# A graph network's rounds on one Trainium2 core: casting and splitting a batch of messages one step earlier, and one-hots and weights ahead between the rounds

## The reference

```python
x = layernorm(x + sage(x))   # 3 x: segment_sum(h[src], dst)/max(cnt,1) @ Wl + bl + h @ Wr, relu between
x = layernorm(x + gin(x))    # segment_sum(gelu(x[src] + edge_attr @ bond_W + bond_b) * ew, dst) + (1+eps)*x, then an MLP 128-256-128
x = layernorm(x + gcn(x))    # 2 x: segment_sum(norm * (h @ W)[src], dst) + self loop + b, relu, layer_norm * g + be
x = layernorm(x + rgcn(x))   # 2 x: segment_sum((h @ W[type])[src], dst) + h @ loop_w + b, relu between
```

## Time and profile before

| | us |
|---|---|
| runs of the kernel: median of 3 | 6575.37 (6567.12 to 6603.21) |
| the profiled execution | 6578.35 |
| its span | 6576.5 |
| rounds 0, 1, 2 (SAGE), by windows | 669, 523, 778 |
| round 3 (GIN) | 895 |
| rounds 4, 5 (GCN) | 748, 983 |
| rounds 6, 7 (RGCN) | 965, 1015 |
| busy in the span: PE, PEld, DVE, ACT, POOL | 4754.8, 3068.4, 3341.3, 2416.9, 1892.9 |

### The profile page before, as it was taken

One profiled execution on the slowest core, in us unless ns is written; L12 is line 12 of the kernel. 1 busy time (PEld: TensorE's weight loads), 2 busy tenths in 40 slices (PEclk: granted clock), 3 DMA queues, 4 the chain that ended last, 5 costly groups with the idle time before them and its releaser, 6 DMA issues. The chain is left out here.

```text
span 6576.5 us, 128477 instructions
## 1 busy us (share of the span) xinstructions
PE 4754.8 (72%) x25114; PEld 3068.4 (47%) x25115; DVE 3341.3 (51%) x10494; ACT 2416.9 (37%) x4967; POOL 1892.9 (29%) x1886
## 2 busy tenths in 40 slices
PE   5879578555577888956676666676788886777776
PEld 3445344222344555534443334342666663666663
DVE  3334233344554555546666566665344442566666
ACT  1333233133325777625554344443122222122223
POOL 4440652443204333034420432200322211322210
PEclk9989889777788999978888788888899999898899
DMA  3543465244323444334442344332233323233323
GB/s 99 160 154 134 154 193 189 94 126 128 127 94 122 142 140 143 128 100 137 137 127 91 113 130 131 123 124 92 88 103 104 98 97 113 84 97 98 100 91 100
DMA packets 429800, 789.83 MB, mean 120 GB/s; under 512 B 69304, under 2 KB 75250, under 8 KB 429716
## 3 DMA queue, kind: packets, MB, share of 16 engines
q1 hardware_dynamic: 375060, 671.58, 30.3%
q0 software_dynamic: 54656, 117.32, 7.2%
HBM read 480.10 MB, written 308.53 MB: 120 GB/s over the span
## 5 line engine op out<-in xcount | busy, mean ns | idle before, releaser
L1048 PE MATMUL p_agg<-onehot,msg 128*128 128x512 f16 (+1 forms) x2848 | 1217.2, 427 | 983.6 <-DVE onehot L1456 685.6
L642 POOL DMA_INDIRECT raw<-node_s,src_i x980 | 937.0, 956 | 2125.9 <-DVE msg L1447 952.7
L1456 DVE TENSOR_SCALAR onehot<-iota,dst_f,negbase 128x512 f16<-128x512 f16 (+1 forms) x2848 | 1063.1, 428 | 639.3 <-issue 232.8
L1050 PE MATMUL p_agg<-onehot,msg 128*128 128x512 f16 (+1 forms) x2848 | 1223.4, 430 | 0.5 <-issue 0.4
L1048 PEld LDWEIGHTS p_agg<-onehot,msg 128*128 x2848 | 292.2, 103 | 1385.4 <-issue 1258.3
L1447 DVE TENSOR_TENSOR msg<-raw,msg x140 | 163.1, 1165 | 728.5 <-ACT msg L763 660.0
L1507 DVE BATCH_NORM_STATS2 stats<-v_ring 128x6 f32 (+1 forms) x1960 | 429.1, 280 | 202.2 <-ACT v_ring L841 94.0
L642 POOL DMA_INDIRECT raw<-node_x,src_i x392 | 380.2, 970 | 430.0 <-issue 421.4
L833 ACT ACTIVATE o<-v_ring,nmr,rstd 128x128 f32 (+1 forms) x1176 | 472.2, 482 | 65.0 <-DVE nmr L1523 53.7
L803 ACT ACTIVATE u<-p_agg,sage_bias 128x512 f32<-128x512 f32 x196 | 133.8, 683 | 795.3 <-PE p_agg L1081 434.7
L1434 DVE SCALAR_TENSOR_TENSOR hid<-type_in,p_wide 128x512 f32<-128x512 f32 x448 | 253.2, 615 | 333.3 <-PE p_wide L1028 205.4
(11 more groups left out here) (258 smaller groups left out, 7953.6 us busy)
## 6 DMA issues: line engine op xcount, KB each, us to landing
node_s<-o SPq DMA_DIRECT2D x392, 256.0 KB
feature<-u SPq DMA_DIRECT2D x294, 256.0 KB
h_in<-feature SPq DMA_DIRECT2D x294, 256.0 KB
node_x<-o SPq DMA_DIRECT2D x294, 256.0 KB
res_in<-node_x SPq DMA_DIRECT2D x294, 256.0 KB
h_in<-node_x SPq DMA_DIRECT2D x196, 256.0 KB
h_in<-node_s SPq DMA_DIRECT2D x196, 256.0 KB
h_t<-dinv_scratch SPq DMA_DIRECT2D x196, 256.0 KB
```

What stands on the lines that cost most here:

```text
L642: nc.gpsimd.indirect_dma_start(out=raw[:, (e % RING) * BATCH + j, :], out_offset=None, in_=src_d, in_offset=bass.IndirectOffsetOnAxis(ap=s ...
L1048: nc.tensor.matmul(p_agg[:, a, :], tile_ap(msg, t, 0, D), oh, start=first, stop=True, skip_group_check=True)
L1050: return nc.tensor.matmul(p_agg[:, a, :], tile_ap(msg, t, D, 2 * D), oh, start=False, stop=True, skip_group_check=True)
L1456: return V.tensor_scalar(tile_ap(onehot, slot), iota[:, :], dst_f[:, bass.ds(t, 1)], negbase[:, bass.ds(it * 2 + a, 1)], ALU.subtract, ALU ...
```

## The change

It alters the order of work; every computation on data stays.

- In the SAGE and GCN rounds ScalarE casts at the head of step `it` the batches of pair `it + 2` instead of `it + 1`, and VectorE splits them at the end of step `it`; pair 1's batches are taken in step 0 too. TensorE's program has a wait for the early batches in all rounds. The list's word now counts on at most three batches a step (`AHEAD`); for these data the words stay as they are. GIN and RGCN keep the place of their batches.
- `onehots` is parted: `first_onehots` (the three of each half) and `more_onehots`. The additional groups of a pair's second half move to the head of VectorE's next step (`next_items`).
- Between the rounds VectorE waits for TensorE's last sums of the round before (`out_done`) and then makes the first six one-hots, before the first batch is split.
- SyncE loads the weights of rounds 3 to 7 ahead of the last store of the round before (`next_weights`), and GIN's 14 bond loads at the start of round 1. The first load of GIN's edge attributes goes ahead of `all_stored`.
- GpSimd hands batch 1 over ahead of the gathers of batch 2.
- In the GCN rounds ScalarE takes `relu_out` of both halves of the last pair ahead of `scale_rows`.

```diff
@@ words and lists
-        def even_list(eng, kind, row):
-
-            items, (first, second, third) = pair_list(eng, kind, row)
-            return (batch_in_word(eng, first), batch_in_word(eng, third)), items
+        def later_list(eng, kind, row):
+
+            items, (first, second, third) = pair_list(eng, kind, row)
+            return (batch_in_word(eng, second), batch_in_word(eng, first), batch_in_word(eng, third)), items
...
-        def batch_list(eng, kind, it):
-
-            end, begin = packed(words[0:1, bass.ds(it * 2 + 1, 2)], kind)
+        def batch_list(eng, kind, pair):
+
+            end, begin = packed(words[0:1, bass.ds(pair * 2 - 1, 2)], kind)
@@ SyncE
+                def next_weights():
+
+                    if r + 1 == len(rounds) or rounds[r + 1].kind == SAGE:
+                        return
+                    wait(sp, q.rows_done, NHALF)
+                    if k == 4:
+                        wait(sp, q.gained, NPAIR)
+                    for dst_ap, src_ap in round_weights(rounds[r + 1]):
+                        sp.dma_start(dst_ap, src_ap).then_inc(R[r + 1].weights_in, 16)
...
                 load(0, 0)
                 load(0, 1)
+                if r == 1:
+                    for dst_ap, src_ap in bond_weights:
+                        sp.dma_start(dst_ap, src_ap).then_inc(bond_in, 16)
...
-                for dst_ap, src_ap in round_weights(rd):
-                    sp.dma_start(dst_ap, src_ap).then_inc(s.weights_in, 16)
@@ GpSimd
-                    if e > 1:
+                    if e > 2:
                         hand_over(e - 1)
-                    elif e == 0:
-                        hand_over(0)
+                    elif e < 2:
+                        hand_over(e)
@@ ScalarE
                 def batches(it):
-                    if exists(it + 1):
-                        each_batch(act, *batch_list(act, PT, it), batch)
+                    if rel or k == 3:
+                        if exists(it + 1):
+                            each_batch(act, *batch_list(act, PT, it + 1), batch)
+                        return
+                    if is_zero(it):
+                        each_batch(act, *batch_list(act, PT, 1), batch)
+                    if exists(it + 2):
+                        each_batch(act, *batch_list(act, PT, it + 2), batch)
...
                 def step(it):
                     batches(it)
                     if k >= 4:
-                        relu_out(it - 1, 1)
+                        if not is_last(it - 1):
+                            relu_out(it - 1, 1)
                         deviation(it - 1)
+                        if is_last(it):
+                            relu_out(it, 0)
+                            relu_out(it, 1)
                         if k == 4:
                             scale_rows(it - 2)
@@ TensorE
-                if rel or k == 3:
-                    end = early_batches(pe, PT, batch)
-                    wait_apart(pe, q.lo_done, end * (1 + rel))
+                end = early_batches(pe, PT, batch if rel or k == 3 else None)
+                wait_apart(pe, q.lo_done, end * (1 + rel))
@@ VectorE
+                def next_items(it):
+
+                    if not exists(it + 1):
+                        if exists(it):
+                            more_onehots(it, 1, single_list(dve, PT, it * 2 + 1))
+                        return None, None, None
+                    if rel or k == 3:
+                        these, (now, after) = odd_list(dve, PT, it * 2 + 1)
+                        each_batch(dve, *these, batch)
+                        ahead = None
+                    elif exists(it + 2):
+                        (e0, e1, e2), (now, after) = later_list(dve, PT, it * 2 + 1)
+                        if is_zero(it):
+                            each_batch(dve, e0, e1, batch)
+                        ahead = (e1, e2)
+                    else:
+                        now, after = pair_list(dve, PT, it * 2 + 1)[0]
+                        ahead = None
+                    more_onehots(it, 1, now)
+                    return after[:3], after[3], ahead
...
                 def gcn_step(it):
-                    if exists(it + 1):
-                        these, (now, after) = even_list(dve, PT, it * 2 + 2)
-                        each_batch(dve, *these, batch)
-                        onehots(it + 1, 0, now)
+                    now, after, ahead = next_items(it)
+                    if now:
+                        onehots(it + 1, now)
                     scaled_sums(it, 1)
                     statistics(it - 1, 1)
                     gain_and_shift(it - 2)
-                    if exists(it + 1):
-                        onehots(it + 1, 1, after)
+                    if now:
+                        first_onehots(it + 1, 1, after)
                     scale_and_move(it - 1)
                     statistics(it, 0)
                     scaled_sums(it + 1, 0)
                     if k == 5:
                         second_scale_and_move(it - 2)
+                    batches_ahead(ahead)
...
+                if r:
+                    wait(dve, S[r - 1].out_done, NHALF)
+                now, after = pair_list(dve, PT, 0)[0]
+                first_onehots(0, 0, now[0])
+                first_onehots(0, 1, after[0])
                 if k == 3:
                     embedded_sum(0)
                 early_batches(dve, PT, batch)
-                now, after = pair_list(dve, PT, 0)[0]
-                onehots(0, 0, now)
-                onehots(0, 1, after)
+                more_onehots(0, 0, now)
```

More of the change, by code:

```diff
@@ L32 @@
 MORE = 2
+AHEAD = RING - 1
 REL = 8
@@ L325, in round_weights @@
                         (one_eps[:, :], rep("L1_gnn_eps"))]
-                for j in range(BATCH):
-                    out.append((bond[j * DE:(j + 1) * DE, j, :], A["L1_gnn_bond_W"]))
-                    out.append((bond[BATCH * DE:BATCH * DE + 1, j, :], A["L1_gnn_bond_b"].partition_broadcast(1)))
                 return out
@@ L345, in build_gnn @@
         sage_weights_in = sem("sage_weights_in")
+        bond_weights = [(bond[j * DE:(j + 1) * DE, j, :], A["L1_gnn_bond_W"]) for j in range(BATCH)]
+        bond_weights += [(bond[BATCH * DE:BATCH * DE + 1, j, :], A["L1_gnn_bond_b"].partition_broadcast(1))
+                         for j in range(BATCH)]
+        bond_in = sem("bond_in")
         shared = {name: sem(name) for name in StepSemaphores.NAMES}
@@ L357, in is_zero, with is_last @@
             return isinstance(it, int) and it == 0
+        def is_last(it):
+            return isinstance(it, int) and it == NPAIR - 1
         def exists(it):
@@ L476, in early_batches @@
             end = eng.snap(((word >> 24) & 31).with_bounds(min_val=1, max_val=BATCHES))
-            with eng.Fori(0, end) as e:
-                body(e.with_bounds(min_val=0, max_val=BATCHES - 1))
+            if body:
+                with eng.Fori(0, end) as e:
+                    body(e.with_bounds(min_val=0, max_val=BATCHES - 1))
             return end
```

54 lines of the change are left out of this document (35 added, 19 removed).

## The result

The changed kernel took 6479.84 us in the median of four runs (6458.47 to 6481.21), the kernel before 6571.24 us in runs beside it. The ratio is 0.9846 with a 95% interval from 0.9805 to 0.9887. The forecast was 6270 us, 305 us less than before; 91 us came by the medians, 97 by the spans of the two profiled executions.

What follows compares the result with a forecast made beforehand. No engine fills the batch cycles; VectorE's wait for ScalarE's cast and TensorE's for one-hots stand in them. 249 us for batches plus 56 around them, 305 us, gave 6270 us (chance 0.53), range 6110 to 6480.

Steps and rivals of the forecast that it cites:

- The cast and split ahead: Rounds 0, 1, 2, 4, 5: gains of 84, 39, 35, 10 and 81 us over 28 batches each, 249 us.
- The moved one-hot groups: Head of VectorE's next step, mostly last steps: adds and statistics go first; gain 12 us, between loss 12 and gain 30.
- The starts and batch 1: Round starts: first one-hots and weights earlier, 24 us; batch 1 handed over earlier in five rounds, 20 us.
- A: Rival: TensorE gets one-hots in time, but other engines see its results at GpSimd's scaling; gain 135 us, 6440 us; chance 0.21.
- the hold: While GpSimd gathers a batch, TensorE's completions reach other engines late, 5.9 us in round 2; the change only moves it.
- B: Rounds 2, 4, 5: GpSimd's scaling meets VectorE at every batch, 2.1 us each; 176 us less gain, 6446 us; chance 0.05.
- C: Rival: everything a batch costs in rounds 0, 1 and 5 goes, 403 us; 504 us in all, 6071 us; chance 0.10.
- D: Rival: ScalarE waits longer for matmuls at each batch, as GpSimd pauses less; 87 us slower, 6660 us; chance 0.07.
- E: Rival: batches aren't there when cast, ScalarE waits in VectorE's stead, only the starts gain; 6555 us; chance 0.04.

Runs made afterwards that it cites:

- e3: The kernel before with the cast and split ahead and nothing else; 6357.78 us, one run.
- e7: e1 with the gathers of batches 4 to 27 left out in the SAGE and GCN rounds, so it computes something else; 5968.93 us, one run.
- e6: e1 with the list read behind the copy of the first half's sum in SAGE, on another chip; 6240.77 us, 0.96 of the kernel before there.
- e10: The changed kernel itself, run again on a third chip; 6483.77 us, 0.9852 of the kernel before.
- e11: The kernel of e6, run again on a third chip; 6330.92 us, 0.9614 of the kernel before.
- e1: The changed kernel with the second half's additional one-hot groups back in their old place; 6320.53 us, 0.9611 of the kernel before.
- e5: The changed kernel with the moved groups at the end of VectorE's step, ahead of the list, on another chip; 6340.19 us, one run, 0.974 of the kernel before.
- e12: e11 with batch 1 handed over behind the gathers of batch 2 again; 6355.66 us, one run.
- e4: The kernel before with only the changes between rounds, batch 1's early handing over and the last pair's order in GCN; 6593.41 us, one run.

## Why the prediction was wrong

**The cast and split ahead.** The mechanism was right for the most part, as the waits and e3 show. The sum over 24 batches a round was near, 231 us measured (220 in e3) against 213 forecast, but that is luck, since the terms were off both ways; and for all 28 batches e3 has 214 against 249. For 24 batches I had 72, 34, 30, 9 and 70 us; measured were 47, 30, 31, 32 and 92. In round 0 TensorE's wait for one-hots did go, 3.4 us a batch, but the cycle is only (35.1 - 31.2)/2 = 2.0 us a batch shorter; unnamed waits came in its place, 229 us where there were 27. What the gathers cost in all e7 shows: round 0's cycle is 29.7 us with them (e6, same chip) and 26.1 without. In round 5 the forecast had it that the one-hots' stretching by the scaling "stays as it is". It fell by 34 us, which is more than the 22 that the term was short; its steps are 16.3 us in the mean, where a step without a batch was 15.49. In round 4 I took too much off the wait for the cast: 31 us came of the 75 that the wait held for 24 batches, where I had 9. Whether the list's reading of 1.68 us, which I subtracted, lay beside another wait, no run shows.

**The moved one-hot groups.** This is the step that failed. The forecast said that they "let the adds and statistics go first", a gain of 12 us between a loss of 12 and a gain of 30, since "no row has this by itself". They cost about 150 us: 153 between e10 and e11, 159 between the medians of the changed kernel and e1. The term was put at a gain of 12, and no rival had such a loss. I had asked whose work gets out of the queue's way, and not who waits for what is moved. TensorE takes the second half's groups at the beginning of its step; they were there already in the kernel before. With the groups at the head of VectorE's next step, TensorE waits until VectorE's whole step and the list are over (5.61 us in the timeline), and VectorE's next sum waits for TensorE. e5 parts the cost: in the last steps 57% is the list's reading ahead of the groups, in the whole time under half, the rest the place. It hits the rounds in which the groups bound the last steps, rounds 3 and 7 too, of which the forecast said that they stay as long as before, and not rounds 0, 1 and 6.

The price could have been bounded from rows that I had. The list was 1.68 us; as an estimate, a later group is late by that at least in each of the nine last steps, 76 us in the five rounds in which VectorE and TensorE turned out to work in turns, and 120 if it were all eight. I used that row for five other terms and not for this one.

**The starts and batch 1.** Forecast 24 + 20 us. The starts are 23 us shorter in the changed kernel, up to the fourth step mark, 15 of it in rounds 6 and 7. There e12 gives up to 17 us to batch 1, in rounds that I had left out of its term; in the five rounds for which I had 20 us it shows nothing. The six one-hots made ahead bring little, because the first batch is the bound. At the start of round 5 of the changed kernel, against the 3629.03 of the earlier trace rows:

```profile
3571.44 2.19 DVE L1486 TENSOR_SCALAR onehot<-iota,dst_f,negbase 128x512 f16<-128x512 f16 x6 [1.22 <-issue]
...
3577.11 0.95 ACT L785 ACTIVATE msg<-raw  x1 [16.81 <-POOL raw L726]
3578.42 1.09 DVE L1481 TENSOR_TENSOR msg<-raw,msg  x1 [4.78 <-ACT msg L785]
...
3580.75 0.61 PE L1081 MATMUL p_agg<-onehot,msg 128*128 128x512 f16 x1 [41.68 <-issue]
```

The one-hots are done 4.8 us before the split begins, and TensorE's first matmul comes 1.2 us after the split's end. What e4 lost in the middle of rounds 0 and 3 stays open in part, as said there.

**The rivals.** A (the hold takes what the cast gave) is true of a part: its sign, longer waits for a releaser not named, came in rounds 0 and 1, which gave 47 and 30 us all the same. B had a mechanism that is real, but with the wrong sign for this change: its full price, a one-hot of 2.4 us once a batch, stood in round 5 of the kernel before, and the change took most of it away. What is left is 0.36 us a batch. C's idea of a batch that costs nothing is what e7 has in rounds 0 and 1, without the gathers. D and E didn't come; the loss came by a mechanism that I hadn't among them. That the time lies inside the range from 6110 to 6480 us, by less than 1 us, is luck, since that end was worked out from A. The clock follows: 0.96 in round 0's window where it was 0.92, and 0.84 in round 4's last steps where it was 0.96. The Trainium skill, TensorE: Matmul & The Clock Gate, HAM oscillation — how this bites in real kernels, has it that repeated pauses of the engine bring the slow clock back each time; the trace agrees for the pause of 5.61 us, after which a matmul took 0.61 us, and in e1, with 1.27 us there, it took 0.39. Not every pause does it: in e5's round 4 two of 4.02 and 4.01 us were followed by 0.61 and 0.39.

The three terms as measured are 231 us in the middle and 23 at the starts, less 106 us in the last steps of five rounds, 31 in the middles of rounds 3, 6 and 7, and 20 in what is left (25 lost behind the last steps, 5 won in the last steps of rounds 0, 1 and 6). That makes 97 us, which is the difference of the two spans. Of the 31, 13 are round 3's, which e1 and e4 have without the moved groups, and some 10 of round 7's 16 are the groups' (e10 less e11).

## What to carry to other kernels

When work is moved in one engine's order, ask first who waits for the moved work and from when, and only then who gets ahead of it. A change with several parts can hold its gain and its loss apart in place: step lengths by stage (middle, last steps, starts) show at once which part to take back. Here the version with the groups left in place runs at 0.961 of the kernel before, where the change as made has 0.985.

## What the runs showed of the hardware

TensorE's completions reach VectorE and ScalarE late while GpSimd works through a run of indirect gathers: in round 2 the unnamed waits come to some 100 us at the add and 210 at the output in 36 steps, with and without the scaling, and to nothing without the gathers. At the add they end 2.6 to 2.8 us after the start of the last gather of the run. Whether the issuing or the transfers do it, no run tells. In all, the gathers cost 43, 91 and 45 us in the 36 steps of rounds 0, 1 and 2 on one chip (e7 against e6), 8 in round 5, and nothing in round 4 (458 us with them, 467 without).

A VectorE instruction that meets GpSimd's scaling of 1.70 us is stretched by up to its whole length: a split of 1.09 us took 2.78 us in round 1 of the kernel before, and 21 one-hots of some 0.4 us took 2.4 to 2.5 us in round 5. VectorE's statistics beside the same scaling took no longer (278 ns in the mean in both kernels' windows of round 5).

The same kernel on two chips (e6 and e11) differs by 1.4%, and not evenly. In one profile of each the 36 steps take 356 and 382 us in round 0, 312 and 336 in round 1, 598 and 628 in round 3, but 484 and 484 in round 2, 458 and 457 in round 4, 586 and 586 in round 5. Kernels are only to be compared by the kernel before on their own chip.
